# A two-block transformer on one core: expert work by token halves, with the next block's first half moved in among it

## What is computed

```python
x = x + L0_xattn(layernorm(x), ctx)     # cross attention, 8 heads of 64
x = x + L0_ffn(layernorm(x))            # 8 experts, the two best of each token
x = x + L1_xattn(layernorm(x), ctx)     # cross attention, 16 heads of 8, with biases
x = x + L1_ffn(layernorm(x))            # three layers of +1/-1 weights, relu between

# L0_ffn: logits = xf @ Wg; top_w = softmax(two best); combine = weight of each expert, or 0
h = einsum('nc,ech->enh', xf, W1)       # 128 -> 256, for every expert
g = einsum('nc,ech->enh', xf, W2)
y = einsum('enh,ehc->enc', silu(h) * g, W3)
out = einsum('enc,ne->nc', y, combine)
```

## Time and profile before

| what | value |
|---|---|
| runs | 233.78 us median of 3 (233.52 to 233.9) |
| the profiled execution | 234.19 us by the same clock as the runs |
| its span, first to last instruction | 232.1 us |
| TensorE busy in the span | 223.3 us, 96% |
| VectorE busy | 166.9 us, 72% |
| ScalarE busy | 120.6 us, 52% |
| GpSimd busy | 70.0 us, 30% |
| one gate, silu, query copy, query stack | 0.69, 0.60, 0.69, 0.70 to 0.75 us |
| statistics of a half, guess, refining | 0.9, 1.0, 1.4 us |
| granted TensorE clock | 1.000, the 2.4 GHz level, throughout |

### The profile page before, as it was taken

The page is one execution under the profiler, slowest core; times in us unless marked ns, Lnnn a source line. Parts: engine busy times, 40 slices in busy tenths (PEclk is TensorE's granted clock), DMA queues, the critical chain, the costliest instruction groups (busy, mean ns, idle before and its releaser), DMA issues.

```text
span 232.1 us, 5028 instructions
## 1 busy us (share of the span) xinstructions
PE 223.3 (96%) x1825; PEld 186.4 (80%) x1825; DVE 166.9 (72%) x433; ACT 120.6 (52%) x288; POOL 70.0 (30%) x105
## 2 busy tenths in 40 slices
PE   8999998899899999999999999999999999989994
PEld 8878887798886788988898889877688887766783
DVE  1677757898977795546555657988788788598862
ACT  2575948697853553223322334165655656757642
POOL 5624599124410305844042910342000000220200
PEclk9999999999999999999999999999999999999999
DMA  6970001000000002202202072000000000000003
GB/s 158 241 195 5 1 3 47 3 0 0 3 0 3 0 6 64 71 0 68 63 5 68 25 201 71 1 3 0 0 3 3 3 0 3 0 3 1 0 0 90
DMA packets 11868, 8.18 MB, mean 35 GB/s; under 512 B 3012, under 2 KB 11144, under 8 KB 11848
## 3 DMA queue, kind: packets, MB, share of 16 engines
q1 hardware_dynamic: 11848, 7.91, 12.7%
HBM read 5.81 MB, written 0.52 MB: 27 GB/s over the span
## 4 chain that ended last, share of the span: by engine, by line
PE 82%; ACT 8%; DVE 7%; issue 1%; POOL 0%; DVEq 0%; ACTq 0%; POOLq 0%
PE ps L676 12%; PE ps L478 9%; PE ps L850 9%; PE ps L480 9%; PE ps L479 9%; ACT probs L984 7%; PE ps L795 4%; PE ps L767 4%; PE ps L754 3%; PE ps L474 3%; PE ps L566 3%; PE ps L485 2%; PE ps L555 2%; PE ps L469 2%; DVE probs L1309 2%; PE ps L544 2%
## 5 line engine op out<-in xcount | busy, mean ns | idle before, releaser
L1041 ACT ACTIVATE kT<-ps 128x512 f32<-128x512 f32 x32 | 19.1, 598 | 47.2 <-PE ps L480 47.2
L676 PEld LDWEIGHTS ps<-w,kT 128*128 128x128 f32 x256 | 30.9, 192 | 1.2
L676 PE MATMUL ps<-w,kT 128*128 128x128 f32 x256 | 31.0, 275 | 0.0
L1385 DVE TENSOR_TENSOR kT<-ps,kT 128x512 f32<-128x512 f32 x32 | 21.8, 688 | 11.1 <-PE ps L480 8.8
L1392 DVE SCALAR_TENSOR_TENSOR x_sb<-ps,comb,x_sb 128x128 f32<-128x128 f32 x64 | 18.0, 342 | 13.5 <-PE ps L676 13.5
L478 PE MATMUL ps<-xT_hi,w_hi 128*128 128x512 f32 x64 | 26.7, 417 | 0.2 <-DVE kT L1385 0.2
L480 PE MATMUL ps<-xT_hi,w_lo 128*128 128x512 f32 x64 | 25.2, 393 | 0.0
L479 PE MATMUL ps<-xT_lo,w_hi 128*128 128x512 f32 x64 | 25.0, 390 | 0.0
L984 ACT ACTIVATE probs<-ps,negmax 128x128 f32<-128x128 f32 x64 | 22.6, 412 | 1.8 <-DVE negmax L1297 1.8
L1479 DVE TENSOR_REDUCE probs<-ps 128x8 f32<-128x1024 f32 x16 | 19.4, 1223 | 4.3 <-PE ps L754 4.3
L415 POOL TENSOR_TENSOR w_hi<-w_raw,zero 128x512 fp32r<-128x512 f32 x8 | 9.3, 1166 | 43.1 <-DMA w_raw<-in_L_ffn_W 28.4
(11 more groups left out here) (208 smaller groups left out, 511.1 us busy)
## 6 DMA issues: line engine op xcount, KB each, us to landing
w_raw<-in_L_ffn_W SPq DMA_DIRECT2D x16, 128.0 KB, 2.2
k_st<-h_a SPq DMA_DIRECT2D x12, 128.0 KB, 2.6
w<-in_L_ffn_W SPq DMA_DIRECT2D x8, 128.0 KB, 2.2
x_sb<-in_x SPq DMA_DIRECT2D x2, 256.0 KB, 5.1
ctx_sb<-in_ctx SPq DMA_DIRECT2D x2, 192.0 KB, 3.4
w_raw<-in_L_xattn_Wq SPq DMA_DIRECT2D x1, 256.0 KB, 5.1
wo<-in_L_xattn_Wo SPq DMA_DIRECT2D x1, 256.0 KB, 5.1
k_i<-in_L_ffn_k SPq DMA_DIRECT2D x1, 256.0 KB, 3.4
```

The costliest lines, as they stand in the source:

```text
L676: ins = pe.matmul(ps[:, 4 + slot, k * C:(k + 1) * C], uT[:, slot, c, k * P:(k + 1) * P], w3[:, buf, c, :], start=(c == 0), stop=(c == NH - 1))
L1041: act.activation(silu[:, c, :], ps[:, c, :], ACT.Silu).then_inc(b_silu, 1)
L1385: dve.tensor_tensor(uT[:, slot, c, :], ps[:, 2 + c, :], silu[:, c, :], ALU.mult).then_inc(b_u, 1)
```

## The change

1. **Order of units.** Experts 0 and 1 still run on both halves; then experts 2 to 7 run on half 0 alone (units 4 to 9), and then 7, 6, 5, 4 on half 1 from the weights that are still there, and 3 and 2 on half 1 from weights that are loaded and split a second time (`JOBS`, ten loads for eight experts). Experts 4 to 7 need four places: two new ones are h_a's second half and, for `W3`, the output weights `wo0` of the first attention. All loops of this stage are written out.
2. **Half 0 of the second attention amid the units of half 1.** Statistics, guess and refining stand on VectorE behind the adds of units 9 and 10, the scale on ScalarE behind unit 12, the transposes inside unit 13, queries 0 and 1 in and behind unit 14, query 2 inside unit 15, query 3 between the last two `b_down`. Their ScalarE and VectorE steps are placed likewise; the exp table is loaded between queries 2 and 3.
3. **New first steps** of the second attention, with 22 `keep_busy` products in five places (`RAMP`).
4. **GpSimd.** The splits of experts 2 and 3 wait for the second half's `xT_lo` instead of for hidden products of unit 1; `k_st` is filled once the gate's weights are there (`b_acc`).

The diff, cut to its core:

```diff
+        RAMP = (12, 3, 3, 2, 2)
...
+        JOBS = (0, 1, 2, 3, 4, 5, 6, 7, 3, 2)
+        SLOT = (0, 1, 2, 3, 0, 1, 2, 3, 3, 2)
+        UNITS = ((0, 0), (0, 1), (1, 0), (1, 1), (2, 0), (3, 0), (4, 0), (5, 0), (6, 0), (7, 0),
+                 (7, 1), (6, 1), (5, 1), (4, 1), (8, 1), (9, 1))
+        NU = len(UNITS)
+        LAST = tuple(max(q for q in range(NU) if UNITS[q][1] == t) for t in range(NT))
+        def done_before(j):
+            return max(q for q in range(NU) if UNITS[q][0] < j and SLOT[UNITS[q][0]] == SLOT[j]) + 1
+        def turn_of(j):
+            return sum(SLOT[i] == SLOT[j] for i in range(j + 1))
...
+        def down_w(j):
+            s = SLOT[j]
+            return w3[:, s, :, :] if s < 2 else wo0[:, 2 * (s - 2):2 * (s - 2) + 2, :]
...
-            return n if n < NG else 5 + 2 * (n % 2)
+            return M0 + 1 - n % 2 if n < NG else 5 + 2 * (n % 2)
...
-            with sp.Fori(1, E // 2) as i:
...
+            sp.wait_ge(a_wo, NB)
+            for j in (2, 3):
+                load_down(j)
+            for j in range(4, len(JOBS)):
+                sp.wait_ge(b_lo, j - 1)
+                load_up(j)
+                sp.wait_ge(b_y, done_before(j))
+                load_down(j)
...
-            def split_expert(e, buf):
-                pool.wait_ge(ld_up[buf], (e - buf) * 16 + 32)
...
-                pool.tensor_tensor(w12_hi[:, buf, :], w12[:, buf, :], zero[:, :].to_broadcast([P, 2 * HID]),
-                                   ALU.add).then_inc(b_hi, 1)
-                pool.wait_ge(b_hi, e + 1)
-                pool.tensor_tensor(w12_lo[:, buf, :], w12[:, buf, :], f32(w12_hi[:, buf, :]), ALU.subtract).then_inc(b_lo, 1)
-            split_expert(0, 0)
-            split_expert(1, 1)
+            def split_up(j):
+                pool.wait_ge(ld_up[j % 2], 32 * (j // 2 + 1))
+                if j >= 4:
+                    pool.wait_ge(b_g, NH * done_before(j))
+                pool.tensor_tensor(up_hi(j), w12[:, j % 2, :], zero[:, :].to_broadcast([P, 2 * HID]), ALU.add).then_inc(b_hi, 1)
+                pool.wait_ge(b_hi, j + 1)
+                pool.tensor_tensor(up_lo(j), w12[:, j % 2, :], f32(up_hi(j)), ALU.subtract).then_inc(b_lo, 1)
...
-            pool.wait_ge(a_wo, NB)
-            for buf in range(2):
-                split_expert(2 + buf, buf)
+            pool.wait_ge(ln_lo, 2 * NT)
+            split_up(2)
+            split_up(3)
+            pool.wait_ge(b_acc, NT)
             pool.wait_ge(masks, 6)
             pool.tensor_copy(k_st[:, :, :].rearrange("p g n -> p (g n)"),
                              is_lo[:, 1:2].to_broadcast([P, NG * NB * P])).then_inc(k1_fill, 1)
+            split_up(4)
+            split_up(5)
             pool.wait_ge(ld_d, 16 * 6)
             pool.tensor_scalar(d1_w[:, :, :], k1_u[:, :, :], 2.0, -1.0, ALU.mult, ALU.add).then_inc(d_w, 1)
             pool.tensor_scalar(d2_w[:, :, :], k2_u[:, :, :], 2.0, -1.0, ALU.mult, ALU.add).then_inc(d_w, 1)
-            with pool.Fori(2, E // 2) as i:
-                for buf in range(2):
-                    split_expert(i * 2 + buf, buf)
+            split_up(6)
+            split_up(7)
             pool.memset(top_w, 0.0).then_inc(zeros_ok, 1)
             chain(pool.memset(qo[:, :, :, :], 0.0))
             chain(pool.memset(v_a[:, :, :, D1:D1 + 1], 1.0))
             pool.wait_ge(v1_ok, NT)
             pool.tensor_copy(v_a[:, :, :, 0:D1], v1.rearrange("p b (h d) -> p b h d", d=D1)).then_inc(c_v, 1)
+            split_up(8)
+            split_up(9)
...
+            def b_down(q):
+                j, slot = UNITS[q][0], q % 2
+                pe.wait_ge(ld_down[SLOT[j]], 16 * turn_of(j))
                 pe.wait_ge(b_u, q * NH + NH)
+                if q >= 2:
+                    pe.wait_ge(b_acc, NT + q - 1)
...
-            for n in range(NG):
-                c_queries(n)
+            for q in range(NU - 2):
+                b_down(q)
+                b_hidden(q + 2, (0,))
+                if q + 2 == LAST[0] + 4:
+                    ln_transposes(2, 0)
+                if q + 2 == NU - 2:
+                    c_queries(0)
+                elif q + 2 == NU - 1:
+                    c_queries(2)
+                b_hidden(q + 2, (1,))
+                if q + 2 == NU - 2:
+                    c_queries(1)
+            b_down(NU - 2)
+            c_queries(3)
+            b_down(NU - 1)
             pe.wait_ge(k1_st, NK1)
-            keep_busy(6, M0)
             c_scores(0, 0)
             c_scores(0, 1)
-            keep_busy(5, M0)
+            keep_busy(RAMP[0], M0)
             c_scores(1, 0)
+            keep_busy(RAMP[1], M0)
+            c_turn_max(0)
+            keep_busy(RAMP[2], M0)
+            c_shifted(0, 0)
+            keep_busy(RAMP[3], M0)
+            c_scores(1, 1)
+            keep_busy(RAMP[4], M0)
             ln_transposes(2, 1)
-            keep_busy(2, M0)
-            c_turn_max(0)
-            keep_busy(2, M0)
-            c_scores(1, 1)
-            for s in range(NB + 2):
+            c_shifted(0, 1)
+            c_turn_max(1)
+            c_scores(2, 0)
+            c_queries(NG)
+            c_values(0, 0)
+            c_queries(NG + 1)
+            c_scores(2, 1)
+            for s in range(1, NB + 2):
                 c_step(s)
             for n in range(4, len(D_ORDER) - 1):
...
+            for q in range(2, NU):
+                b_silu_step(q, (0,))
+                if q == LAST[0] + 4:
+                    ln_hi_copy(2, 0)
+                b_silu_step(q, (1,))
+                if q == LAST[0] + 3:
+                    ln_scale(2, 0)
+                if q == NU - 2:
+                    c_query_signed(0)
+                    c_query_signed(1)
+            c_query_signed(2)
+            table(ACT.Exp)
+            c_query_signed(3)
...
-            act.wait_ge(ln_nm, 1)
-            for b in range(4, NB):
-                act.activation(xn[:, b, :], x_sb[:, b, :], ACT.Identity, bias=nm[:, b:b + 1],
-                               scale=rs[:, b:b + 1]).then_inc(ln_xn, 1)
+            ln_scale(2, 1)
+            c_exp_half(0, 0)
             ln_hi_copy(2, 1)
-            for s in range(NB + 1):
+            c_exp_half(0, 1)
+            c_query_signed(NG)
+            c_query_signed(NG + 1)
+            for s in range(1, NB + 1):
...
-                q, e = i * 4, i * 2
-                b_add(q, 0, e, 0, q + 1)
...
-                b_add(q + 3, 1, e + 1, 1, q + 4)
-                b_gate(q + 5, 1)
-            q = 2 * E - 4
-            b_add(q, 0, E - 2, 0, q + 1)
-            b_gate(q + 2, 0)
-            b_add(q + 1, 1, E - 1, 0, q + 3)
-            dve.wait_ge(b_acc, q + 4)
-            for b in range(4):
-                ln_stats(b)
-            b_gate(q + 3, 1)
-            ln_root(2, 0)
-            ln_scale(0)
-            b_add(q + 2, 0, E - 2, 1, q + 3)
...
-            for n in range(NG):
-                c_query_stack(n)
+            for q in range(NU - 2):
+                unit_add(q)
+                if q == LAST[0]:
+                    unit_stats(0)
+                if q == LAST[0] + 1:
+                    ln_refine(0)
+                    newton(dve.tensor_tensor(nm[:, 0:4], meanvar[:, 0:4, 0], rs[:, 0:4], ALU.mult))
+                    dve.tensor_scalar(nm[:, 0:4], nm[:, 0:4], -1.0, None, ALU.mult).then_inc(ln_nm, 1)
+                b_gate(q + 2, q % 2, (0,))
+                if q == LAST[0] + 2:
+                    ln_low(2, 0)
+                if q + 2 == NU - 2:
+                    c_query_stack(0)
+                b_gate(q + 2, q % 2, (1,))
+                if q + 2 == NU - 2:
+                    c_query_stack(1)
+                if q == LAST[0]:
+                    ln_seed_only(2, 0)
+            c_query_stack(2)
+            unit_add(NU - 2)
+            c_query_stack(3)
+            unit_add(NU - 1)
+            unit_stats(1)
+            ln_seed_pool(2, 1)
             dve.wait_ge(zeros_ok, 1)
             c_top(0, 0)
             c_top(0, 1)
+            c_shift(0)
             c_top(1, 0)
-            c_shift(0)
+            c_top(1, 1)
             ln_low(2, 1)
-            c_top(1, 1)
-            for s in range(NB + 2):
+            c_shift(1)
+            c_top(2, 0)
+            c_query_stack(NG)
+            c_top(2, 1)
+            c_query_stack(NG + 1)
+            for s in range(1, NB + 2):
                 c_step(s)
             d_low(3)
```

155 lines of the change are left out of this document (52 added, 103 removed).

## The result

The changed kernel takes 234.34 us, median of 11 runs (233.92 to 235.4), against 233.52 for the kernel before in the same rounds (11 runs, 233.43 to 233.9). The ratio is 1.0037, 95% interval 1.0022 to 1.0052: 0.8 us slower, where 0.6 us faster was forecast. The time lies inside the whole range of 232.1 to 234.8, but on the wrong side of no change, and outside the 232.8 to 233.8 that the forecast gave itself.

The account below looks back on a forecast made before the run. TensorE was taken to bound the kernel, busy 223.3 of 232.1 us. Gains of 0.26 us up to the mark and 0.3 at the gates, 0.56 together, took 233.78 to 233.2 us; whole range 232.1 to 234.8.

Parts of the forecast that it names:

- g: Gates ahead of unit 2: earlier splits free VectorE's `gd` sooner, gaining 0.3 us (0.05 to 0.45).
- The 16 units stay: 0.: Expert stage on TensorE: the same 16 units in another order, priced at no change.
- T0: End of the last `b_down`, where scores can start: 146.82 plus queries, transposes and switches, 151.0 us less g.
- T0 to the mark: Second attention, from T0 to the third transposition of maxima (batch 2): 17.9 us, reaching 168.9 less g against 169.16.
- units with moved work: Units 11 to 15, given half 0's steps: no stall, 0 us, with 0.7 us of cover at unit 12.
- exp table: ScalarE, between queries 2 and 3: load takes 1.5 us in all; scores start without a wait, by 0.14 us.
- Rival 3: Units with moved work: a step is asked for too early and a unit stalls, 234.3 us; chance 0.12.
- Rival 1: Gates: the bias steps lose whole splits, `lg` 1.9 late, unit 2 1.2 later, 234.7 us; chance 0.14.
- Rival 2: Way into the second attention: shorter than laid out, its chain closing 1 us earlier, 232.2 us; chance 0.22.
- Rival 4: Second attention: early scores' lead wholly waited away, mark at 169.16 or a little later, 233.8 us; chance 0.10.

Follow-up runs that it names:

- Runs 4 and 5: Sigmoid ahead of the key copies on ScalarE: in the changed kernel 233.84 us, ratio 1.0016; in the kernel before 233.66 us, ratio 0.9988.
- run 6: Kernel before with the halves of the expert weights kept in h_a's second row instead of tile w12: 234.43 us, ratio 1.0013.
- run 3: Changed kernel with the three bias steps moved on VectorE behind the adds of unit 4: 234.28 us, ratio 1.0032 to the kernel before.
- run 2: Changed kernel with GpSimd's splits of experts 2 and 3 waiting for unit 1's hidden products again: 237.7 us, ratio 1.0152 to the kernel before.
- run 7: Changed kernel with fillers 12, 2, 3, 2, 0 instead of 12, 3, 3, 2, 2: 233.6 us, ratio 0.9992 to the kernel before.

## Why the prediction was wrong, step by step

- **g, the gates: the step that failed first.** I followed the chain `lg`, `gd`, the gate of unit 1, TensorE's unit 2, and forecast 0.3 there; it gave 0.42 at unit 2. But I priced g at the first wait that it shortens and carried it to the end. The same chain has a second branch, `gd`, sigmoid, `gw`, `comb`, adds, gate of unit 2, that runs over ScalarE, and there ScalarE's work (key copies behind TensorE's products) arrived level with VectorE's in the kernel before, so it ended last as soon as VectorE came earlier. What arrived at unit 3 was 85.13 against 85.23: g = -0.1. Runs 4 and 5 show it. Error: 0.4 us.
- **"The 16 units stay: 0."** The weights of eight of them moved to another place in SBUF, and that costs 8 x 0.033 = 0.26 us (run 6). I had bounded the wait and the transfers of the new places, not the pace of products that take their weights from there. Nothing in the trace before showed it for these products.
- **T0's starting point.** The two errors make 0.66, but the scores came only 0.53 later than forecast. Two small ones nearly close that. I took 146.82 for the end of the last `b_down`, which is where its modelled duration ends; the next product starts at 146.58, 0.24 earlier, as the row below shows. Against that, the transposes and the four queries cost 4.25 us and not 4.2, and the last `b_down` took 1.88 us up to the first scores and not 1.79. That my starting point was late is luck: it hid a part of the other errors.

```profile
146.58 0.94 PE L474 MATMUL ps<-ones_r,ones 128*128 128x512 f32 x3
```

- **T0 to the mark, 17.9 us; measured 18.3.** The steps up to query 4 were right to 0.1: transposes of half 1 due at T0 + 9.5 came at 160.18 - 150.76 = 9.42, query 4 due at + 11.7 came at + 11.72. Then a query between other products takes 1.13 us (162.48 to 163.61, 164.19 to 165.32) and not 0.93, which is its pace among queries: two of them are the 0.4. (In between, one wait for maxima takes up 0.1 of it, and the step behind gives it back.) I had used, queries one behind the other, though the trace before has such a lone query too, 1.13 us from its first product to the scores behind it:

```profile
164.31 0.50 PE L478 MATMUL ps<-xT_hi,wq_hi 128*128 128x512 f32 x1
...
165.44 0.33 PE L754 MATMUL ps<-k_st,h_c 32*128 32x128 f32 x2
```

- **The units with moved work did not stall**, the transposes and queries cost nearly what they should (0.47 and 0.92 us, the lone query ahead of the last `b_down` 1.01), scores start right behind the last `b_down`, and the exp table is hidden by about what was computed; the row's price for the table was right, and the drain of about 1.38 us that the Trainium skill (ScalarE: Activation LUTs, "What ACT_TABLE_LOAD costs") adds did not appear. After, a load begins at 79.48 and the sigmoid at 80.78, 1.30 us on. Rival 3 is out for the units that I feared, but the wait ahead of unit 3 is of its kind, at a place I had not looked at.
- **Rival 1** had its mechanism: two of three bias steps lost a whole split. It did not reach its deciding point, `lg` 0.7 late (0.15, and run 3 shows no cost). The Trainium skill (SBUF — State Buffer, "SBUF: two separate sides") says that on the port pair which VectorE and GpSimd share, the one that starts first keeps it for its whole instruction. The 1.26 and 1.24 us agree with that, and so does `gw` at 1.02 in run 2.
- **Rival 2** was worth half of what I gave it: the chain closes 0.5 us earlier, once fillers go (run 7), not by itself. **Rival 4** has what happened: the lead of the scores is wholly waited away and the mark is a little later. Its 233.8 is 0.5 short of the median, and that rival 3's 234.3 lies next to it is luck.
- The sum, in the spans: forecast -0.56; g 0.4 less, place 0.26, queries 0.4, together +0.5, against a measured +0.35 to +0.37. The remaining 0.1 lies within the small errors at T0's starting point and the reading of the shift. The median adds what the longer executions and the time around the span add, which no step had.

## What to carry to other kernels

When a step is made earlier, follow **every** branch that leaves it to the point where they meet again, and on each ask which engine ends last; the gain is what the slowest branch passes on, here nothing until ScalarE served the sigmoid before the key copies. A branch that arrives level with the one that is made earlier is the one to look for: it shows no wait before the change. Reordering work among engines' queues is only finished when each queue serves the new critical chain first: two small edits (the sigmoid ahead of two copies, three fillers fewer) turned 0.4% slower into 0.3 to 0.4% faster. And fillers are sized for one order; after a reorder, count again which of them end behind the moment at which the next product's input is ready.
